# Column sums in compact form, spreads in one pass, squares of new slots on ScalarE

## The reference

```python
# slots = layernorm(x): 4096 tokens of 256 features; P = context, 4 x 64 tokens
Pn = rmsnorm(P, input_norm_w); k_proj = Pn @ Wk.T; v_proj = Pn @ Wv.T
for _ in range(3):
    sn = rmsnorm(slots, slot_norm_w)
    q_proj = sn @ Wq.T
    scores = einsum('bkd,bmd->bkm', q_proj, k_proj) * SCALE
    attn = softmax(scores, axis=-2)                    # over the 1024 tokens of a batch
    attn = attn / (sum(attn, axis=-1) + EPS)           # over the 64 context tokens
    updates = einsum('bkm,bmd->bkd', attn, v_proj)
    slots = gru_cell(updates, slots, ...)
x = x + tanh(g_xattn) * slots
x = x + tanh(g_ffn) * ffn(layernorm(x))                # 16 experts, 512 tokens each, and a shared one
```

## Time and profile before

| what | us |
|---|---|
| median of 3 runs | 1280.48 (1280.4 to 1283.75) |
| the profiled execution | 1288.91 |
| its span | 1287.1 |
| PE busy over the span | 1153.2 (90%), 6000 instructions |
| DVE busy | 888.7 (69%) |
| ACT busy | 579.6 (45%) |
| POOL busy | 415.8 (32%) |
| mean granted PE clock | 0.938 of full speed |

### The profile page before, as it was taken

One profiled execution on the slowest core, in us unless ns is written; L12 is line 12 of the kernel. 1 busy time (PEld: TensorE's weight loads), 2 busy tenths in 40 slices (PEclk: granted clock), 3 DMA queues, 4 the chain that ended last, 5 costly groups with the idle time before them and its releaser, 6 DMA issues. The chain is left out here.

```text
span 1287.1 us, 17969 instructions
## 1 busy us (share of the span) xinstructions
PE 1153.2 (90%) x6000; PEld 961.8 (75%) x6000; DVE 888.7 (69%) x1513; ACT 579.6 (45%) x866; POOL 415.8 (32%) x321
## 2 busy tenths in 40 slices
PE   5569989899999865899987799999999999999995
PEld 4446767676767754688876688888888888888884
DVE  7586888878778669677893566666666666666662
ACT  4244545454535426322343554545444544544441
POOL 4241333333310014233354123333333333332341
PEclk9659999998999987899989799999999999999998
DMA  4300000000000034300002544344444444444421
GB/s 150 87 8 10 9 9 9 8 5 11 0 17 9 9 131 132 106 17 33 17 33 82 206 114 123 99 117 127 126 131 131 131 104 110 123 127 127 131 34 17
DMA packets 45603, 95.58 MB, mean 74 GB/s; under 512 B 11008, under 2 KB 36864, under 8 KB 41216
## 3 DMA queue, kind: packets, MB, share of 16 engines
q1 hardware_dynamic: 31808, 75.98, 17.6%
q0 software_dynamic: 12288, 17.31, 8.0%
q10 hardware_dynamic: 1472, 1.84, 0.4%
HBM read 74.11 MB, written 17.07 MB: 71 GB/s over the span
## 5 line engine op out<-in xcount | busy, mean ns | idle before, releaser
L1863 DVE SCALAR_TENSOR_TENSOR ehid<-eup,b_up,esilu 128x512 f32<-128x512 f32 x128 | 96.1, 751 | 180.8 <-PE eup L1732 160.7
L1700 POOL DMA_INDIRECT out_tokens<-yo,idx_out x64 | 113.3, 1770 | 243.2 <-DVE yo L1837 228.6
L1786 ACT ACTIVATE esilu<-egate,b_gate 128x512 f32<-128x512 f32 x128 | 87.6, 685 | 154.5 <-PE egate L1732 153.5
L1745 PE MATMUL edown<-w_hi,eh_hi 128*128 128x256 f32 x512 | 145.3, 284 | 0.0
L1745 PE MATMUL edown<-w_hi,eh_lo 128*128 128x256 f32 x512 | 144.3, 282 | 0.0
L1745 PE MATMUL edown<-w_lo,eh_hi 128*128 128x256 f32 x512 | 143.0, 279 | 0.0
L1795 ACT ACTIVATE eh_hi<-ehid 128x512 fp32r<-128x512 f32 x128 | 81.0, 633 | 116.9 <-DVE ehid L1863 116.9
L1815 DVE TENSOR_TENSOR w_lo<-raw,w_hi 128x768 fp32r<-128x768 f32 x128 | 121.2, 949 | 7.8 <-ACT w_hi L1775 7.8
L522 PE MATMUL gate_banks<-slots_hi,whh_hi 128*128 128x512 f32 x288 | 119.4, 414 | 4.6 <-ACT tr L660 4.5
L522 PE MATMUL gate_banks<-slots_hi,whh_lo 128*128 128x512 f32 x288 | 116.6, 405 | 0.0
L522 PE MATMUL gate_banks<-slots_lo,whh_hi 128*128 128x512 f32 x288 | 116.3, 404 | 0.0
(11 more groups left out here) (278 smaller groups left out, 2743.0 us busy)
## 6 DMA issues: line engine op xcount, KB each, us to landing
raw<-in_w_expert SPq DMA_DIRECT2D x32, 1536.0 KB
token_rows<-work SPq DMA_DIRECT2D x8, 512.0 KB, 3.2
out_tokens<-y SPq DMA_DIRECT2D x8, 512.0 KB, 3.0
attn<-attn_lo SPq DMA_DIRECT2D x24, 128.0 KB, 2.3
work<-in_x SPq DMA_DIRECT2D x4, 512.0 KB, 4.9
raw<-in_x SPq DMA_DIRECT2D x4, 512.0 KB, 6.1
b_down<-in_down_b SPq DMA_DIRECT2D x1, 2048.0 KB, 7.2
raw<-in_w_shared SPq DMA_DIRECT2D x1, 1536.0 KB, 10.3
```

The source lines that it names most:

```text
L1700: pool.indirect_dma_start(out, bass.IndirectOffsetOnAxis(idx_out[:, j:j + 1], 0), yo[:, j, :], None, compute_op=ALU.add).then_inc(g_add, 16)
L1745: last = nc.tensor.matmul(edown[:, j // 2, (j % 2) * D:(j % 2 + 1) * D], h[:, f % RING, tok], w[:, f, 4 * P:6 * P], start=(f == 0 and m == ...
L1786: nc.scalar.activation(esilu[:, f % 2, :], egate[:, f % 2, :], ACT.Silu, bias=b_gate[:, bass.ds(e, 1), f:f + 1].rearrange("p a b -> p (a b ...
L1863: nc.vector.scalar_tensor_tensor(ehid[:, f % 2, :], eup[:, f % 2, :], b_up[:, bass.ds(e, 1), f:f + 1].rearrange("p a b -> p (a b)"), esilu ...
```

## The change

It has six parts. (1) The column sums are made compactly: eight matmuls, each with a 128x128 block of `expo` loaded and the 128x2 `rsum` moving, write 128x16 values beside the transposed ones in the bank of `rms_b`; DVE adds the epsilon and takes one reciprocal of 128x16; PE transposes them (`turn_rec`, within unit (3,0)), DVE multiplies with `own_block`, and PE spreads them into `score` (`spread_rec`, behind unit (3,0)). ACT's copies of the sums are gone. (2) Both spreads are one-pass: the small values are split in a high and a low part (`two_parts`), on partitions 0 to 15 and 32 to 47 of one 128-row tile. (3) The low part of the attention is written by DVE straight to the other partitions; SP's transfers go. (4) ACT squares the new slots behind `nn` (`squares`); POOL makes the low part of the slots first and then adds. (5) The last sum of squares stands between the two halves of the scores. (6) ACT's `attention_hi` of half 0 moves from before unit (3,1) into it, DVE's `attention_half` and `attention_lo` move by one place. The setup has four more selects and a copy of `pick_group`.

```diff
@@ -98,3 +98,6 @@
-        own_block = asb("own_block", [GPP * BLK, BLK, P])
-        pick_group = asb("pick_group", [GPP * BLK, 2, P])
-        half_mask = asb("half_mask", [P, P])
+        NB = GPP * BLK
+        LOW = 32
+        NR = LOW + NB
+        own_block = asb("own_block", [NR, BLK, P])
+        pick_group = asb("pick_group", [P, 2, P], F32R)
+        batch_mask = asb("batch_mask", [P, 2])
@@ -255,6 +261,9 @@
+                act.wait_ge(c_pool, C_PICK)
+                for r in (0, LOW):
+                    nc.scalar.activation(pick_group[r:r + NB, :, :], pick_f[:, :, :], ACT.Copy)
@@ -274,34 +283,37 @@
-                for j in range(GPP):
+                for j in (*range(GPP), *range(LOW // BLK, LOW // BLK + GPP)):
...
@@ -421,15 +433,17 @@
-            attn_lo = lsb("attn_lo", [P, GROUP], F32R)
-            spread = lsb("spread", [GPP * BLK, BLK, P])
-            rsum = lsb("rsum", [P, P])
+            spread = lsb("spread", [P, BLK, P], F32R)
+            rsum = lsb("rsum", [P, 2])
+            csum_e = lsb("csum_e", [P, NB])
+            rec = lsb("rec", [P, NB])
+            rms_parts = lsb("rms_parts", [P, P])
+            rec_parts = lsb("rec_parts", [P, P])
...
+            csum_t = rms_b[:, P:P + NB]
@@ -486,19 +502,6 @@
             def _(sp):
                 for g in range(G1, G):
...
-                def move_low(s, pair, h):
-                    sp.wait_ge(v_alo, 2 * s + h + 1)
...
-                        sp.dma_start(attn[rows_of(1 - b), pair, b, h * GROUP:(h + 1) * GROUP].bitcast(F32),
-                                     attn_lo[rows_of(b), :].bitcast(F32)).then_inc(d_alo, 16)
@@ -533,7 +536,7 @@
                     def wait_attention():
...
-                        pe.wait_ge(d_alo, 32 * (4 * it + 2 * pair + g4 % 2 + 1))
+                        pe.wait_ge(v_alo, 4 * it + 2 * pair + g4 % 2 + 1)
@@ -560,9 +563,13 @@
                     from_attention(gate_x, 4 + c, True).then_inc(m_x, 1)
-                def scores(s, pair, split_before):
+                def scores(s, pair, split_before, last_squares=None):
+                    if last_squares is not None:
+                        pe.wait_ge(v_attn, 2 * s)
...
+                        if h == 1 and last_squares is not None:
+                            last_squares()
@@ -592,9 +599,22 @@
                 def column_sums(s):
...
+                    for c in range(2 * BLK):
+                        last = nc.tensor.matmul(csum_t.rearrange("p (b c) -> p b c", b=2)[:, :, c],
+                                                expo[:, c * P:(c + 1) * P], rsum[:, :], start=True, stop=True)
+                    last.then_inc(m_csum, 1)
+                def turn_rec(s):
+                    pe.wait_ge(v_recd, s + 1)
+                    nc.tensor.transpose(rms_b[:, 0:P], rec_parts[:, :], ident[:, :]).then_inc(m_rect, 1)
+                def spread_rec(s):
+                    pe.wait_ge(v_dia2, s + 1)
...
-                        nc.tensor.matmul(score[:, h, :], rsum[:, :], expo[:, h * GROUP:(h + 1) * GROUP],
-                                         start=True, stop=True).then_inc(m_csum, 1)
+                        nc.tensor.matmul(score[:, h, :], pick_group[:, h, :], spread[:, :, :].rearrange("p b t -> p (b t)"),
+                                         start=True, stop=True).then_inc(m_rec, 1)
                 def half_iteration(it, pair, softmax, more):
@@ -620,7 +639,9 @@
                         column_sums(s)
...
-                    gru_unit(it, pair, 3, 0)
+                    gru_unit(it, pair, 3, 0, (lambda: turn_rec(s)) if softmax else None)
+                    if softmax:
+                        spread_rec(s)
                     gru_unit(it, pair, 3, 1)
@@ -669,12 +692,21 @@
+                    if after is not None:
+                        after()
                 def slots_high(it, pair, g4):
...
+                def squares(it, pair, g4):
+                    g = pair * GPP + g4
+                    act.wait_ge(s_ss, it * G + g + G - 1)
+                    nc.scalar.activation(square[:, g % 2, :, :], slots[:, :, tokens(pair, g4)],
+                                         ACT.Square).then_inc(s_sqa, 1)
                 def copy_rms(s, h):
@@ -684,12 +716,6 @@
-                def copy_csum(s):
-                    for h in range(2):
-                        act.wait_ge(m_csum, 2 * s + h + 1)
-                        nc.scalar.activation(csum_c[:, h, :], score[:, h, :], ACT.Identity,
-                                             bias=attn_eps[:, :]).then_inc(a_csum, 1)
                 def attention_hi(s, pair, h):
@@ -702,7 +728,7 @@
                     def high(p, g4):
-                        return (lambda: slots_high(it, p, g4)) if more else None
+                        return ((lambda: slots_high(it, p, g4)), (lambda: squares(it, p, g4))) if more else ()
@@ -711,28 +737,24 @@
-                        gru_unit(it, pair, 0, 0, last_high)
+                        gru_unit(it, pair, 0, 0, last_high, lambda: squares(it - 1, 1, GPP - 1))
...
-                        gru_unit(it, pair, 0, 0, high(0, GPP - 1))
+                        gru_unit(it, pair, 0, 0, *high(0, GPP - 1))
...
                     gru_unit(it, pair, 0, 1)
-                    gru_unit(it, pair, 1, 0, high(pair, 0))
+                    gru_unit(it, pair, 1, 0, *high(pair, 0))
...
                     gru_unit(it, pair, 1, 1)
...
-                    gru_unit(it, pair, 2, 0, high(pair, 1))
+                    gru_unit(it, pair, 2, 0, *high(pair, 1))
...
                     gru_unit(it, pair, 2, 1)
-                    if softmax:
-                        copy_csum(s)
-                    gru_unit(it, pair, 3, 0, high(pair, 2))
-                    if softmax:
-                        attention_hi(s, 1 - pair, 0)
-                    gru_unit(it, pair, 3, 1)
+                    gru_unit(it, pair, 3, 0, *high(pair, 2))
+                    gru_unit(it, pair, 3, 1, (lambda: attention_hi(s, 1 - pair, 0)) if softmax else None)
@@ -806,19 +827,30 @@
                     def do(ins):
...
-                        ins.then_inc(v_rms if n[0] < 11 else v_rmsd, 1)
-                        if n[0] < 11:
-                            dve.wait_ge(v_rms, s * 10 + n[0])
+                        ins.then_inc(v_rms, 1)
+                        dve.wait_ge(v_rms, s * 11 + n[0])
...
+                    two_parts(s, rms_parts, rms, v_hi16, v_rmsd)
+                def two_parts(s, parts, full, v_high, v_done):
+                    high, low = parts[:, 0:NB].bitcast(F32R), parts[:, LOW:NR].bitcast(F32R)
+                    nc.vector.tensor_copy(high, full[:, :]).then_inc(v_high, 1)
+                    dve.wait_ge(v_high, s + 1)
+                    nc.vector.tensor_tensor(low, full[:, :], parts[:, 0:NB], ALU.subtract).then_inc(v_done, 1)
+                def own_columns(done):
+                    nc.vector.tensor_tensor(
+                        spread[0:NR, :, :], own_block[:, :, :],
+                        rms_b[0:NR, 0:P].rearrange("p (a q) -> p a q", a=1).to_broadcast([NR, BLK, P]),
+                        ALU.mult).then_inc(done, 1)
                 def spread_steps(s):
...
-                    nc.vector.tensor_tensor(
-                        spread[:, :, :], own_block[:, :, :],
-                        rms_b[0:GPP * BLK, 0:P].rearrange("p (a q) -> p a q", a=1).to_broadcast([GPP * BLK, BLK, P]),
-                        ALU.mult).then_inc(v_diag, 1)
+                    own_columns(v_diag)
                 def scale_scores(s, h):
@@ -836,28 +868,34 @@
-                    nc.vector.tensor_scalar(rsum[:, :], half_mask[:, :], rden[:, :], None, ALU.mult).then_inc(v_rsum, 1)
+                    nc.vector.tensor_scalar(rsum[:, :], batch_mask[:, :], rden[:, :], None, ALU.mult).then_inc(v_rsum, 1)
                 def half_of(h):
...
-                def csum_reciprocal(s, h, part):
-                    dve.wait_ge(a_csum, 2 * s + h + 1)
-                    cols = slice(part * GROUP // 2, (part + 1) * GROUP // 2)
-                    nc.vector.reciprocal(csum_c[:, h, cols], csum_c[:, h, cols]).then_inc(v_rec, 1)
+                def csum_reciprocal(s):
+                    dve.wait_ge(m_csum, s + 1)
+                    nc.vector.tensor_scalar(csum_e[:, :], csum_t, ATTN_EPS, None, ALU.add).then_inc(v_rec, 1)
+                    dve.wait_ge(v_rec, 2 * s + 1)
+                    nc.vector.reciprocal(rec[:, :], csum_e[:, :]).then_inc(v_rec, 1)
+                    dve.wait_ge(v_rec, 2 * s + 2)
+                    two_parts(s, rec_parts, rec, v_rech, v_recd)
+                def spread_reciprocal(s):
+                    dve.wait_ge(m_rect, s + 1)
+                    own_columns(v_dia2)
                 def attention_half(s, h):
-                    dve.wait_ge(v_rec, 4 * s + 2 * h + 2)
-                    nc.vector.scalar_tensor_tensor(expo[:, half_of(h)], expo[:, half_of(h)], rden[:, :], csum_c[:, h, :],
+                    dve.wait_ge(m_rec, 2 * s + h + 1)
```

(45 more changed lines are left out.)

41 lines of the change are left out of this document (18 added, 23 removed).

## The result

The change made the kernel slower: 1290.78 us median (1290.38 to 1291.84, 5 runs) against 1281.88 us (1280.4 to 1284.32) for the kernel before, ratio 1.0069 with a 95% interval of [1.0054, 1.0085]. The forecast was 1277, faster, range 1267 to 1286: wrong in sign and outside the range.

What follows compares the result with a forecast made beforehand. PE was taken to bound the slot loop (busy 343.0 of 368.0 us). Waits and work saved 7.4 us, the clock cost 3.5, leaving 3.9 less than the median 1280.5: 1277, range 1267 to 1286.

Steps and rivals of the forecast that it cites:

- PE work: Softmax halves: cheaper one-pass spreads, column sums 1.8 us and no gain; net 0.9 us less per half, 4.7 in five.
- The new pause: Behind unit (3,0), PE waits 2.7 us for DVE in five halves; with transpose and spreads 16.5 us more.
- The pauses that go: From a half's start to the rms transpose: DMA, pre and rms waits go, 18.2 us less in all.
- The adds: Before the column sums: GpSimd's add delays DVE by 1.1 us, rsum pause 1.8 instead of 0.7; 3.2 us less remains.
- The last half: At the last half's start PE's wait for tr falls from 4.52 to 1.7 us, gain about 3.0.
- Ahead of the loop: Setup and first softmax: PE 0.5 us later, bounds -1.5 to +1.
- The sum before the clock: Waits and work of all steps together, without clock effects: 7.4 us less.
- The clock: Slot loop: 7 to 8 half-speed falls, 11 us, against 7 lost now and 1 in the last half; net 3.5 worse.
- The base: Profiled run 1288.9 us, timed median 1280.5: the 3.9 us saving computed on the profile was taken off the median.
- Rival B: Column sums to (3,1) in each softmax half: 13 falls, 21 us against 8, so 1286, slower; chance 0.17.

Runs made afterwards that it cites:

- e8_moved: e1_early with column sums behind gate r of unit (3,0), squares behind gate z, and DVE's reciprocal chain within unit (2,1): 1251.34 us.
- e0_before: The kernel before, unchanged, run once more for its profile and clock: 1281.94 us, ratio 0.9997.
- e3_oldsums: The changed kernel with the dense column sums, ACT copies, four DVE reciprocals and attention order of before (parts 1 and 6 undone): 1268.20 us.
- e2_fill: The changed kernel with nine unused one-pass matmuls of 448 columns in the pause ahead of spread_rec: 1283.57 us.
- e1_early: The changed kernel with DVE multiplying the transposed reciprocals before unit (3,0) and not within it: 1270.37 us.
- e11_together: e8_moved with the squares directly behind the column sums again, narrow work in one piece: 1256.47 us.
- e5_fillsum: e1_early with eight unused one-pass matmuls of 448 columns in the rsum pause ahead of the column sums: 1264.77 us.
- e10_direct_fill: The kernel before with only part 3 (DVE's direct write), plus sixteen unused matmuls ahead of the rms transpose in four halves: 1284.88 us.
- e6_expfirst: e1_early with ScalarE's exponential of unit (2,0) ahead of its squares of the new slots: 1271.59 us.

## Why the prediction was wrong, step by step

- **PE work.** Right for the column sums. Eight column-sum matmuls take 1.70 us from start to start (197.85 to 199.55 in e8_moved; 1.8 forecast).
- **The new pause.** Right: 2.59 us from 214.36 + 0.23 to 217.18, five times (2.7 forecast).
- **The pauses that go.** Right for DMA, `pre` and rms in halves two to five. The first half got an rms wait of 1.6 that wasn't foreseen.
- **The adds.** Right: L813 blocked at 1.66, `rsum` pause 1.84 (1.8 forecast). The Trainium skill ("SBUF — State Buffer", Who interferes with whom) says that a VectorE instruction with two SBUF inputs contends with a GpSimd instruction that reads SBUF; L813, which met none before, agrees (1.66 instead of the 0.692 of the earlier trace rows).
- **The last half.** Pause 2.60 against 1.7 forecast. The product of `attention_half` ended 6.2 us after the half's start (416.27 to 422.47) and not 5.3; PE asked after 5.5, as drawn, and `tr` ended 2.0 behind the product (1.9 forecast): 4.52 - 2.60 = 1.9 gained instead of 3.0.
- **Ahead of the loop.** Right: unit (0,0) of the first half starts at 92.4 instead of 91.9, 0.5 lost as forecast.
- **The sum before the clock.** Right in its direction, too small in size. Stretch by stretch against e0_before, with half of the half-speed time taken out of each (an estimate, as a fall also covers waits): from the column sums to the next half 14.6 us more in five (16.5 forecast), from a half's start to the rms transpose 18.8 less (18.2), from there to the column sums 5.2 less (3.2), the last half 1.9 less (3.0), ahead of the loop 0.5 more (0.5). Together 10.8 less, where the forecast had 7.4. So this part erred by 3.4 us in the kernel's favour, and only the clock made the change slower.
- **The clock: the step that failed.** "7 to 8 falls x 1.5 = 11 us, against the 7 lost now and 1 in the last half. Net 3.5 us worse." Measured: 42.1 us at half speed after, 21 us lost, not 11 (1.0 of the 42.1 belongs to a fall that begins ahead of the loop): each of the four 4.4 us stretches drew one, four of the five pauses did and the last half's too, and two of them lasted 6.8 (at 142.4) and 10.2 us (at 333.5) instead of 3.4. And 2 lost in the kernel before, not 8. Net 19, not 3.5 (its own terms, 11 less 8, give 3). What was mis-sized is how often, and for how long, a pause or a thin stretch draws a fall: the forecast took 7 to 8 falls of 3.4 us from a profile in which no pause of the halves with a softmax was longer than 1.9 us.
- **The base.** "I take the difference over" hid the second half of that error. The first profile was 8.4 us above the median, and I suspected that its half-speed stretches were not in the timed runs; then they could not be set against those of the changed kernel. e0_before shows that they were not there (4.2 against 19.5 us). The two loop ends differ by 8.7 us, and the measured terms are how that splits: -10.8 by waits and work, and +19.5 by the clock (half of the 38.9 us by which the half-speed time from the first unit on differs). On the median of the kernel before that is 1281.9 + 8.7 = 1290.6, against 1290.8 timed.

Rival B named the right mechanism and even its size (13 falls, 21 us lost); it too set 8 us against it, and so stopped at 1286, with a chance of 0.17. The Trainium skill ("TensorE: Matmul & The Clock Gate", What's actually happening) says that idleness throttles the array and activity releases it. The forecast cited it as speaking against the change and gave it 2 to 4 us more; the trace of after has a fall at eight of the nine places (not behind the first 2.4 us pause, at 154.3), and e8_moved, with as many narrow matmuls but none of the pauses, shows clock 1.00.

What stays open: why pauses of 1.8 us before dense work (e0_before, e3_oldsums) leave the clock at 1.00 in nearly every half, and why the same place had 3.4 us in one half and 10.2 in another. No run here tells the position of a pause apart from its length. Whether the 0.4 us waits for `tr` in e8_moved can go wasn't tried.

## What to carry to other kernels

Price a pause of a nearly saturated TensorE at more than its length: here a pause of 2.6 us cost 2.6 plus 1.4 of clock (7.2 us in five, e2_fill), and two pauses of 1.8 gathered into one of 4.0, three times over, cost 13 us over the kernel, although the waits added up to only 1 us more. A gain in the busy time of other engines (DVE fell from 888.3 to 849.3 us) brought nothing here until the hand-over to the bound engine was placed so that useful dense work lay in front of it; moving three calls gained 19 us (e1_early to e8_moved), more than parts 2 to 5 together (13.3). And when a single profile stands above the median of the timed runs, take another, or count its extra losses as absent in the base.

## What the runs showed of the hardware

- Narrow matmuls (1 or 2 columns behind a loaded 128x128 block) keep PE "busy" in the profile but not the clock up: 2.5 us of them in one piece brought a half-speed stretch in three of four halves (e11_together), in two pieces with dense work between them in none (e8_moved, halves one to four).
- Dense matmuls without use in a pause saved more than they cost: 7.2 us (e2_fill), 5.6 (e5_fillsum), 9.8 (e10_direct_fill).
- GpSimd blocks even a DVE instruction of 128x2 values: 1.04 us instead of 0.23 (e6_expfirst).
- DVE writing 64 partitions to the other 64 needed no DMA and showed no price of its own: one such instruction of 64x512 takes 0.69 us in after, as long as one within the same partitions took before, and e10_direct_fill ends 0.18% above the kernel before, with the fill's overshoot in it.
